# A post-norm decoder block with experts on one core: weight splits in later search rounds, weighted rows ahead of the last one-hot rows, maxima split once per block

## The reference

```python
x = layernorm(x + state_space(x))        # h = h @ A + u_t @ Bm over 1024 steps, gated, @ W_out
x = layernorm(x + cross_attention(x, ctx))   # 16 heads of 16, 64 keys per batch
# experts choose tokens: 8 experts, each takes its k = 2048 / 8 = 256 best tokens
logits = xf @ Wr + br
Sm = softmax(logits)
G_t, idx_t = top_k(Sm.T, k)
tokens = xf[idx]
mid = silu(tokens @ W_up[group] + b_up)      # group = expert // 2, 256 -> 682
out = mid @ W_down + b_down                  # 682 -> 256
y = zeros.at[idx].add(G * out)
x = layernorm(x + y)
```

## Time and profile before

| what | us |
|---|---|
| median of 3 runs | 309.56 |
| lowest and highest run | 309.16, 309.83 |
| the profiled execution, first to last instruction (span) | 310.0 |
| TensorE busy | 253.1 (82%) |
| VectorE busy | 196.5 (63%) |
| ScalarE busy | 155.0 (50%) |
| GpSimd busy | 134.7 (43%) |

### The profile page before, as it was taken

How to read it: one execution, slowest core, us unless ns; L and a number is a source line. 1 busy time by engine, 2 the same in 40 slices (tenths; PEclk the granted TensorE clock), 3 DMA queues, 4 the chain that set the end, 5 groups by cost and what they waited for, 6 DMA issues and landing times.

```text
span 310.0 us, 5155 instructions
## 1 busy us (share of the span) xinstructions
PE 253.1 (82%) x1695; PEld 204.6 (66%) x1695; DVE 196.5 (63%) x593; ACT 155.0 (50%) x322; POOL 134.7 (43%) x204
## 2 busy tenths in 40 slices
PE   6999999899988999999995111378299999999790
PEld 3754557565556879989893011247299999999780
DVE  1644467278967479767895887750537776775474
ACT  3743302625487455555222477403237987875125
POOL 6806923716353315545222248277272133333033
PEclk9999999999999899999998555557689999999996
DMA  6961021026183818320000799934035845522727
GB/s 177 290 122 24 2 66 39 0 51 152 22 198 81 188 25 178 78 53 0 3 1 0 231 345 390 295 82 113 20 86 137 209 77 114 125 30 30 186 104 271
DMA packets 33403, 35.59 MB, mean 115 GB/s; under 512 B 10338, under 2 KB 25698, under 8 KB 33122
## 3 DMA queue, kind: packets, MB, share of 16 engines
q1 hardware_dynamic: 30002, 31.16, 35.7%
q0 software_dynamic: 2784, 4.00, 7.7%
q10 hardware_dynamic: 592, 0.12, 0.2%
HBM read 18.16 MB, written 8.19 MB: 85 GB/s over the span
## 4 chain that ended last, share of the span: by engine, by line
PE 57%; DVE 12%; ACT 10%; DMA 8%; issue 5%; POOL 4%; another core or an unknown queue 2%; SPq 1%; DVEq 0%; POOLq 0%; ACTq 0%
PE bank L1153 12%; PE bank L1390 8%; PE bank L1592 6%; PE bank L1341 4%; PE bank L1239 3%; PE bank L1310 2%; DVE junk L1942 2%; DMA Y<-summed_rows 2%; PE bank L1377 2%; ACT bank L1097 2%; POOL rstd L783 2%; DMA X<-in_x 2%; DMA WUR<-in_L_ffn_W_up 2%; PE bank L1324 2%
## 5 line engine op out<-in xcount | busy, mean ns | idle before, releaser
L782 POOL TENSOR_SCALAR var_eps<-mean_var 128x1 f32<-128x1 f32 (+2 forms) x37 | 8.5, 230 | 80.8 <-DVE mean_var L1787 80.4
L848 POOL DMA_INDIRECT summed_rows<-OUT,idx x14 | 21.7, 1551 | 35.9 <-DVE OUT L2060 33.4
L1390 PEld LDWEIGHTS bank<-VB,PT 128*128 128x128 f32 x256 | 33.0, 194 | 1.6
L1390 PE MATMUL bank<-VB,PT 128*128 128x34 f32 x256 | 31.4, 270 | 0.0
L1153 PE MATMUL bank<-FTH,WUH 128*128 128x256 f32 x94 | 28.4, 302 | 2.6 <-DVE idx L2036 2.6
L1097 ACT ACTIVATE bank<-bank,b_up_c 128x256 f32<-128x256 f32 (+1 forms) x48 | 19.5, 447 | 19.1 <-PE bank L1153 14.0
L1153 PE MATMUL bank<-FTL,WUH 128*128 128x256 f32 x94 | 27.6, 293 | 0.3 <-issue 0.3
L1153 PE MATMUL bank<-FTH,WUL 128*128 128x256 f32 x94 | 27.6, 293 | 0.0
L1794 DVE TENSOR_REDUCE NMF<-bank 128x8 f32<-128x512 f32 x32 | 21.7, 681 | 7.6 <-PE bank L1353 7.4
L2070 DVE TENSOR_TENSOR ML<-bank,MH 128x512 fp32r<-128x512 f32 x16 | 11.0, 689 | 22.0 <-ACT MH L1103 19.1
L1592 PE MATMUL bank<-WDH,MH 128*128 128x256 f32 x80 | 23.4, 293 | 1.2 <-DVE ML L2074 1.2
(11 more groups left out here) (336 smaller groups left out, 741.2 us busy)
## 6 DMA issues: line engine op xcount, KB each, us to landing
WDR<-in_L_ffn_W_down SPq DMA_DIRECT2D x8, 640.0 KB
QS<-QH SPq DMA_DIRECT2D x32, 128.0 KB, 2.8
WUR<-in_L_ffn_W_up SPq DMA_DIRECT2D x4, 682.0 KB, 5.0
routed_rows<-X SPq DMA_DIRECT2D x2, 1056.0 KB, 10.3
X<-in_x SPq DMA_DIRECT2D x4, 512.0 KB, 5.3
QS<-QL SPq DMA_DIRECT2D x16, 128.0 KB, 2.6
summed_rows<-X SPq DMA_DIRECT2D x2, 1024.0 KB, 9.8
Y<-summed_rows SPq DMA_DIRECT2D x8, 256.0 KB, 5.7
```

The costliest lines, as they stand in the source:

```text
L848: pool.indirect_dma_start(summed, bass.IndirectOffsetOnAxis(ap=idx[:, 2 * e + h:2 * e + h + 1].bitcast(U32), axis=0), OUT[:, (2 * e + h) % ...
L1390: last = pe.matmul(o[:, j * 34:(j + 1) * 34], PT[m % 2][:, j, s * P:(s + 1) * P], VB[:, m // 2, j].rearrange("p h d -> p (h d)"), start=Tr ...
```

## The change

Three edits. The pieces in `beside` are moved: expert group 0's up weights from rounds 2 to 5 to rounds 4 to 7, the down weights of experts 0 and 1 behind them, and the last two pieces of expert 1 come after the last round. On VectorE the last expert's first `middle_low` and the second one-hot matrix now come after `experts_out(6)`, and the sync queue waits for both one-hot matrices ahead of the reload of `Y`. The maxima's high and low parts are made once per block of four tiles from a buffer of four tiles, in one wide operation each.

```diff
             for e in range(E - 1):
                 sp.wait_ge(scattered[e], 32)
+            sp.wait_ge(rows_made, 2)
...
-            beside = {1: (tokens_spread,), 2: (up_high, 0, 0, 0), 3: (up_high, 0, 0, 1), 4: (up_high, 0, 1, 0), 5: (up_high, 0, 1, 1),
-                      6: (down_high, 0, 0), 7: (down_high, 0, 1), 8: (down_high, 0, 2), 9: (down_high, 0, 3),
-                      10: (down_high, 1, 0), 11: (down_high, 1, 1), 12: (down_high, 1, 2), 13: (down_high, 1, 3)}
+            beside = {1: (tokens_spread,), 4: (up_high, 0, 0, 0), 5: (up_high, 0, 0, 1), 6: (up_high, 0, 1, 0), 7: (up_high, 0, 1, 1),
+                      8: (down_high, 0, 0), 9: (down_high, 0, 1), 10: (down_high, 0, 2), 11: (down_high, 0, 3),
+                      12: (down_high, 1, 0), 13: (down_high, 1, 1)}
...
+            down_high(1, 2)
+            down_high(1, 3)
             up_high(1)
             down_high(2)
...
-                pe.wait_ge(nm_made, TPB * (n + 1))
+                pe.wait_ge(nm_made, n + 1)
...
+                if c == 0 and t >= TPB and t % TPB == 0:
+                    dve.wait_ge(nm_made, t // TPB)
                 half = HD // KC
-                dve.tensor_reduce(NMF[:, t % 2, c * half:(c + 1) * half],
+                dve.tensor_reduce(NMF[:, t % TPB, c * half:(c + 1) * half],
...
-            def maxima_high(t):
+            def maxima_high(n):
                 for c in range(KC):
-                    wait_moved(dve, ("mx", t, c))
-                n, s = t // TPB, t % TPB
-                if n >= 2 and s == 0:
+                    wait_moved(dve, ("mx", TPB * n + TPB - 1, c))
+                if n >= 2:
                     wait_filled(dve, ("nmt", n - 2))
-                dve.tensor_copy(NMS[:, n % 2, s, :, 0, :], by_pair(t)).then_inc(nm_hi, 1)
+                dve.tensor_copy(NMS[:, n % 2].rearrange("p s j l h -> p (s j) l h")[:, :, 0, :], by_pair())\
+                    .then_inc(nm_hi, 1)
...
-                if live(g, "mx"):
-                    maxima_high(mx)
+                if live(g, "mx") and mx % TPB == TPB - 1:
+                    maxima_high(mx // TPB)
                 if live(g, "pv"):
                     inverse_sums(pv)
-                if live(g, "mx"):
-                    maxima_low(mx)
+                if live(g, "mx") and mx % TPB == TPB - 1:
+                    maxima_low(mx // TPB)
...
+            def rows_of(h):
+                dve.wait_ge(rows_ready, 2)
+                wait_up_low(dve, NG - 1)
+                dve.tensor_scalar(ROWS[h][:], row_id[:], own_row[:, h:h + 1], None, ALU.is_equal)\
+                    .then_inc(rows_made, 1)
...
                 if step[0] == "up":
-                    middle_low(*step[1:])
+                    if step != ("up", E - 1, 0):
+                        middle_low(*step[1:])
...
-                    if step[2] == 2 and e in (E - 3, E - 2):
-                        h = e - (E - 3)
-                        dve.wait_ge(rows_ready, 2)
-                        wait_up_low(dve, NG - 1)
-                        dve.tensor_scalar(ROWS[h][:], row_id[:], own_row[:, h:h + 1], None, ALU.is_equal)\
-                            .then_inc(rows_made, 1)
+                    if step[2] == 2 and e == E - 3:
+                        rows_of(0)
                 if step[0] == "dn" and e < E - 1:
                     experts_out(e)
+                    if e == E - 2:
+                        middle_low(E - 1, 0)
+                        rows_of(1)
```

More of the change, by code:

```diff
@@ L1792, in maxima, with by_pair, maxima_low @@
                 wait_filled(dve, name)
+                if c == 0 and t >= TPB and t % TPB == 0:
+                    dve.wait_ge(nm_made, t // TPB)
                 half = HD // KC
-                dve.tensor_reduce(NMF[:, t % 2, c * half:(c + 1) * half],
+                dve.tensor_reduce(NMF[:, t % TPB, c * half:(c + 1) * half],
                                   bank_of(name)[:].rearrange("p (h k) -> p h k", k=SE), AX.X, ALU.max,
                                   negate=True).then_inc(sem_moved(name), 1)
-            def by_pair(t):
-                return NMF[:, t % 2, :].rearrange("p (j h) -> p j h", h=2)
-            def maxima_high(t):
+            def maxima_high(n):
                 for c in range(KC):
-                    wait_moved(dve, ("mx", t, c))
-                n, s = t // TPB, t % TPB
-                if n >= 2 and s == 0:
+                    wait_moved(dve, ("mx", TPB * n + TPB - 1, c))
+                if n >= 2:
                     wait_filled(dve, ("nmt", n - 2))
-                dve.tensor_copy(NMS[:, n % 2, s, :, 0, :], by_pair(t)).then_inc(nm_hi, 1)
[L1809 to L1812, removed]
+                dve.tensor_copy(NMS[:, n % 2].rearrange("p s j l h -> p (s j) l h")[:, :, 0, :], by_pair())\
+                    .then_inc(nm_hi, 1)
+            def by_pair():
+                return NMF[:].rearrange("p s (j h) -> p (s j) h", h=2)
+            def maxima_low(n):
+                dve.wait_ge(nm_hi, n + 1)
+                ns = NMS[:, n % 2].rearrange("p s j l h -> p (s j) l h")
+                dve.tensor_tensor(ns[:, :, 1, :], by_pair(), ns[:, :, 0, :].bitcast(F32), ALU.subtract)\
                     .then_inc(nm_made, 1)
```

## The result

| | before | changed |
|---|---|---|
| median of 13 runs each, us | 309.61 | 311.45 |
| span of the profiled execution | 310.0 | 310.0 |
| mean granted clock | 0.904 | 0.905 |
| GpSimd busy | 134.7 | 135.1 |

The ratio is 1.0054, with an interval of 1.0037 to 1.0071: **slower**, by 1.67 us (0.0054 x 309.56). The two spans are the same all the same, and this is the first thing to explain: a run's time is its span plus 1.8 us (the changed kernel's profiled run took 311.84, its span is 310.0), so the profiled execution of before, span 310.0, stood some 2 us above its kernel's median, where the changed kernel's stood 0.4 above its own. The 0.44 us that stand beside the profile before set a span against the time of a run, and so made that execution look usual. The spans can't be compared. The stages can.

What follows compares the result with a forecast made beforehand. It took the waits to run over TensorE in attention and experts, VectorE in the search, last scatter and reload at the end; +1.25 - 0.57 + 0 = +0.68, forecast 310.2 us against median 309.56; range 308.5 to 311.3.

Steps and rivals of the forecast that it cites:

- its likeliest outcome: Whole kernel: slower, chance 0.44, against 0.38 for the same and 0.18 for faster.
- The stall removed, -0.74: Threshold search: a 2.00 us round, with ScalarE's first split waiting for a load, becomes 1.26; search ends 0.74 us earlier.
- the last rival: Search: the stall in round 3 is not the load's; given no weight.
- Part 1: Search: weight splits moved two rounds later; term +1.2 to +1.25 us, +1.25 taken, not -0.74.
- GpSimd's later end and the hold: After the search: GpSimd's low parts end about 1.25 us later and hold VectorE's `eq` and `cig`, delaying the first gather.
- The counterexample that the prediction gave, at 117.28: A small 128x16 VectorE operation not held during a GpSimd operation with one tensor operand; cited against the hold.
- The fast rival (VectorE not held): Search's tail: VectorE isn't held, or GpSimd lets it in between; -0.74 - 0.57 = -1.31, 308.2 us; chance 0.18.
- The tail, -0.57: Last scatters: weighted rows scaled 0.87 us earlier, but the one-hot matrix holds the second issue's start to 284.5; gain 0.57.
- the first rival: Last scatters: the one-hot matrix stops the scatter issues, a loss of 0.3; total +1.55, 311.1 us; chance 0.22.
- the three readings: One-hot matrix beside scatter issues: disturbs nothing, gain 0.87; delays the second issue's start, gain 0.57; stops the first, loss 0.3.
- The maxima, 0: Maxima split once per block: frees 3.8 us of VectorE but changes nothing in time, bounds 0.2 either way.
- The warning about TensorE's clock: First expert: if TensorE's clock comes back up at another moment, all of it shifts; no size given.

Runs made afterwards that it cites:

- The splits alone: Kernel before with only the weight-split pieces in `beside` moved two search rounds later; 311.54 us, ratio 1.0068.
- The deferral: Whole change, with GpSimd's low part of expert 1's down weights moved behind its first twelve gathers; 309.19 us, ratio 0.9988.
- the kernel with all other parts: Kernel before with expert 1's low part deferred, weighted rows first, one-hot matrix early and splits moved: 309.16 us, 0.9959; with maxima by blocks too: 309.12 us, 0.9979.
- the last experiment: Second run of the whole change with the second one-hot matrix made at expert 7's transposes; 311.41 us, ratio 1.0059.
- tail alone: Kernel before with only the order at the last scatters and the sync queue's wait changed; 309.98 us, ratio 1.0019.
- the matrix early: Whole change with the second one-hot matrix made at expert 7's transposes, an expert's length earlier on VectorE; 311.36 us, ratio 1.0058.

## Why the prediction was right or wrong

It forecast +0.68 us, 310.2, slower or no change; measured was +1.67, slower. The sign of its likeliest outcome and the range (309.56 x 1.0054 = 311.2, under 311.3) held; the number was 1.0 too low, and the median of 311.45 by itself lies just over the upper end. That the range held by 0.1 us is luck: two terms were off, and both the same way. By its steps:

**The stall removed, -0.74: the term holds for the execution shown and hardly at all for the kernel.** The load that ScalarE waited for landed late in that one. The step that failed is the reading of one row as a property of the program; the last rival said that this had "no weight", but it had only asked whether the wait was the load's (it was), not how often the load is that late. Part 1 gained nothing against the usual execution, and its term is 29.92 - 27.95 = **+1.97**, where +1.25 was taken. The splits alone measured +2.1.

**GpSimd's later end and the hold: right, in place and in size.** The start of the first chain was forecast at 188.25 and the end of the second at 197.15 to 197.20, counted from a search at 173.29. With the search 0.99 earlier that is 187.26 and 196.16 to 196.21; measured are 187.26 and 196.19. `eq` "over 2 us" was 2.32, `cig` ended 0.28 after GpSimd for 0.29. Against the profile of before, the first distance grew by 1.24, for 1.20 to 1.25. The deferral shows that the hold causes it, since it takes GpSimd's second chain of subtractions away and the loss goes with it. The rule of the Trainium skill (SBUF — State Buffer, section SBUF: two separate sides) on two-input VectorE operations and GpSimd agrees here in `eq` and `cig`: 2.32 and 0.96 beside GpSimd, 0.22 and 0.42 alone. The counterexample that the prediction gave, at 117.28, was not the only one: there are four of the kind in the trace of before, and the one below lies well inside GpSimd's operation.

```profile
120.25 1.24 POOL L806 TENSOR_SCALAR X<-X,mean_var,rstd 128x256 f32<-128x256 f32 x1
120.91 0.13 DVE L1812 TENSOR_TENSOR NMS<-NMF,NMS 128x16 fp32r<-128x16 f32 x1
```

So the hold is shown for GpSimd's subtractions of two tensors, and was not seen beside its operation with one.

**The fast rival (VectorE not held)** falls by the same rows.

**The tail, -0.57: wrong.** The forecast was that the matrix holds the start of the second issue; it holds the end of the running one. That is the mechanism of the first rival, but its size was wrong too. The rival let the issue's remaining 0.56 us follow the matrix, a loss of 0.3. In fact the issue ended 0.08 after the matrix, and the second one starts 13.34 after the first one-hot matrix, where before it was 13.42 (285.32 - 271.98, 285.07 - 271.65). So the term is **-0.1**, and 0.0 at the reload (17.32, 17.29). It lies inside the bounds of -0.87 and +0.3, but near none of the three readings; the pick was the middle one, and its row (a gather that began while VectorE's operation was running) was of another kind of VectorE operation. The warning of the Trainium skill (same section) that GpSimd can't write descriptors while VectorE works on both ports had the direction right. (By the prediction's own terms its first rival comes to 0.4 rather than 0.3: 283.33 + 1.28 + 0.56 + 0.30 = 285.47, against 285.07.)

**The maxima, 0:** not contradicted and not shown. Alone they measured +0.15% with an interval that holds zero, and on the kernel with all other parts +0.20%, inside the intervals too.

**The sum** of the measured terms is +1.97 - 0.1 + 0 = +1.9, against a measured +1.67 with an interval of +1.1 to +2.2. The warning about TensorE's clock, "all of it shifts", was in place as well: it is where one execution of the last experiment lost 1.8 us.

## What to carry to other kernels

When work is moved to a later slot, follow it to its last consumer on every engine and ask what runs beside its new end: here the moved ScalarE copies showed no cost, and the GpSimd chain that waits for them held a single VectorE instruction for 2 us. Put long GpSimd subtractions where VectorE has no two-operand work on the critical path, and a wide single-operand VectorE operation like this one-hot matrix where no indirect DMA's issue is waited for. And before a stall is put into a sum, look at it in a second execution.

## What the runs showed of the hardware

- A VectorE `TENSOR_TENSOR` of 128x128 bf16 took 2.32 us beside a GpSimd subtraction of 1280 columns and 0.22 without; a scan of the same size 0.96 and 0.42. The profile shows the wait as a longer instruction, not as idle time; what gives it away is that the instruction ends 0.08 to 0.29 us after GpSimd's.
- A scatter's issue on GpSimd was 2.33 us beside a 128x2048 int32 comparison of VectorE and 1.54 to 1.55 without. In every case (changed, tail alone, and expert 5's with the matrix early, there 2.17) it ended 0.08 or 0.09 after the comparison, although 0.57 to 0.76 us of it should still have been to go when the comparison began. That reads as if the issue went on beside the comparison up to its last piece, and only that waited; no run here separates the pieces.
- A VectorE subtraction of two SBUF tensors that began with 0.83 us of such an issue to go lengthened nothing, and took the 1.48 us that it takes elsewhere too. In the kernel before:

```profile
268.42 1.54 POOL L848 DMA_INDIRECT summed_rows<-OUT,idx  x1 [0.30 <-issue]
269.13 1.48 DVE L2080 TENSOR_TENSOR WDL<-WDR,WDH 128x1280 fp32r<-128x1280 f32 x1
```

- The same program took 69.44 and 71.26 us for the same stage, with TensorE's return from 1.2 to 2.4 GHz some 3.7 us apart on their timelines. A change of 0.8 us can go unseen in the time beside that.
